# Spectral filter stage: every second group makes all eight filter steps in column tiles, between the sums

## The reference

```
def _stu_conv(phi, u, n):              # phi: (L, 16) filters, u: (b, sl, d)
    Vf = rfft(phi, n);  Uf_p = rfft(u, n);  Uf_m = rfft(u * sgn, n)
    U_plus  = irfft(Vf[None, :, :, None] * Uf_p[:, :, None, :], n)[:, :sl]
    U_minus = irfft(Vf[None, :, :, None] * Uf_m[:, :, None, :], n)[:, :sl] * sgn
def _compute_spectral(u, sigma, phi, Mpp, Mpm):
    s = sigma ** 0.25
    return einsum('btkd,k,kde->bte', U_plus, s, Mpp) + einsum('btkd,k,kde->bte', U_minus, s, Mpm)
def _stu(u, sigma, phi, Mu, Mpp, Mpm): return _compute_spectral(...) + _compute_ar_u(Mu, u)
t = t + _L1_ffn_ref(_ln_t(t), sigma, phi, M_u, M_phi_plus, M_phi_minus, log_weights, gumbel)
```

## Time and profile before

| | us |
|---|---|
| median of three runs | 1867.33 (1863.99 to 1873.28) |
| the profiled execution: its span, first to last instruction (the page gives no other time of it) | 1861.2 |
| median less span | 6.1 |
| TensorE matmuls busy | 1766.9, 95% of the span |
| VectorE busy / ScalarE busy | 1286.2 / 1178.1 |
| GpSimd busy | 623.4 |
| mean granted TensorE clock | 0.981 of full speed |

### The profile page before, as it was taken

How to read it: one execution, slowest core, us unless ns; L and a number is a source line. 1 busy time by engine, 2 the same in 40 slices (tenths; PEclk the granted TensorE clock), 3 DMA queues, 4 the chain that set the end, 5 groups by cost and what they waited for, 6 DMA issues and landing times.

```text
span 1861.2 us, 76300 instructions
## 1 busy us (share of the span) xinstructions
PE 1766.9 (95%) x32475; PEld 1389.6 (75%) x32475; DVE 1286.2 (69%) x3723; ACT 1178.1 (63%) x2555; POOL 623.4 (33%) x799
## 2 busy tenths in 40 slices
PE   5899999999999988989999999999999999999998
PEld 3567676666767656766788888888888888876665
DVE  2677778888877765373577777777777777647665
ACT  5788888888867654323677777777777777630000
POOL 6555555565545442030532213333312233100000
PEclk8999999999999989999999999999999999999999
DMA  4422333433232313598322122212221222277782
GB/s 118 114 79 74 103 85 92 111 90 100 71 105 77 96 52 115 140 224 197 119 60 62 38 67 68 67 47 68 57 58 43 68 67 64 79 184 205 208 207 70
DMA packets 266000, 183.74 MB, mean 99 GB/s; under 512 B 39888, under 2 KB 263022, under 8 KB 263868
## 3 DMA queue, kind: packets, MB, share of 16 engines
q1 hardware_dynamic: 262782, 177.29, 36.5%
q0 software_dynamic: 640, 1.16, 0.2%
q10 hardware_dynamic: 2240, 0.40, 0.1%
HBM read 108.26 MB, written 70.63 MB: 96 GB/s over the span
## 4 chain that ended last, share of the span: by engine, by line
PE 69%; DVE 10%; DMA 6%; issue 4%; POOL 4%; SPq 4%; ACT 3%; DVEq 0%; POOLq 0%; ACTq 0%
PE banks L1368 20%; PE banks L1346 10%; PE banks L1349 9%; PE banks L405 6%; DVE zone L606 3%; PE banks L1185 3%; PE banks L399 3%; SPq L1484 3%; PE banks L364 2%; PE banks L1180 2%; PE banks L354 2%; DMA zone<-Yd 2%; PE banks L412 2%; DMA YL<-Yd 2%; PE banks L1556 2%
## 5 line engine op out<-in xcount | busy, mean ns | idle before, releaser
L1401 DVE COPY Gm<-banks 128x448 f32<-128x448 f32 x896 | 552.8, 639 | 215.4 <-PE banks L1346 135.6
L1387 ACT ACTIVATE Gm<-banks 128x448 f32<-128x448 f32 x896 | 515.8, 629 | 189.9 <-PE banks L1346 144.3
L1368 PE MATMUL banks<-Gm,U 128*32 128x128 f32 x12544 | 515.0, 274 | 8.7 <-issue 7.9
L1368 PEld LDWEIGHTS banks<-Gm,U 128*32 128x32 f32 x12544 | 338.9, 110 | 51.6 <-issue 50.2
L1349 PE MATMUL banks<-V,zone 118*32 118x224 bf16 x7040 | 292.6, 259 | 0.2 <-issue 0.2
L1425 POOL COPY U<-UL 128x896 f32<-128x896 f32 (+2 forms) x28 | 50.1, 1788 | 545.9 <-PE banks L1368 441.0
L1346 PE MATMUL banks<-V,zone 118*128 118x224 bf16 x1824 | 215.0, 260 | 0.8 <-ACT qT L1196 0.6
L868 POOL TENSOR_TENSOR W<-W,mx 128x280 f32<-128x280 f32 x196 | 130.2, 664 | 226.2 <-DVE mx L655 224.9
L1349 PEld LDWEIGHTS banks<-V,zone 118*32 118x32 bf16 x7040 | 193.7, 96 | 0.8 <-issue 0.6
L1346 PEld LDWEIGHTS banks<-V,zone 118*128 118x128 bf16 x1824 | 157.0, 98 | 47.4 <-issue 39.3
L1556 PE MATMUL banks<-YC,zone 98*98 98x256 f32 x768 | 173.8, 387 | 3.8 <-DVE YC L1628 3.8
(11 more groups left out here) (164 smaller groups left out, 2545.6 us busy)
## 6 DMA issues: line engine op xcount, KB each, us to landing
Yd<-YS SPq DMA_DIRECT2D x112, 224.0 KB, 4.3
W<-Vd SPq DMA_DIRECT2D x392, 49.0 KB
zone<-Yd SPq DMA_DIRECT2D x32, 392.0 KB
YL<-Yd SPq DMA_DIRECT2D x32, 392.0 KB
UL<-Ud SPq DMA_DIRECT2D x27, 448.0 KB, 4.1
zone<-Mbf SPq DMA_DIRECT2D x28, 256.0 KB
Vd<-W SPq DMA_DIRECT2D x56, 112.0 KB
T<-XR SPq DMA_DIRECT2D x28, 224.0 KB, 2.6
```

Source lines behind the costliest of these rows:

```text
L1368: ins = e.matmul(p[32 * x:32 * x + 32, :], self.U7[(2 * P + ch) % 3][:, sl, 8 * (3 - q):8 * (3 - q) + 32], self.Gm[:, par, r:r + 2, :], st ...
L1387: e.activation(dst, src, ACT.Copy).then_inc(S["gm_act"], 1)
L1401: v.tensor_copy(dst, src).then_inc(S["gm_dve"], 1)
```

## The change

In groups 1 and 3 of each stage (`j % 2 == 1`) all eight steps are tiled, and they alternate with the parts of the sums: 0 1 p0 2 p1 3 p2 4 p3 5 p4 6 7 p5 p6. Groups 0 and 2 keep the run of four whole steps.

```diff
@@ Filters.order
-                out += step(0) + step(1) + step(2) + step(3) + part(0) + part(1) + step(4) + step(5) + part(2) + step(6)
-                out += part(3) + step(7) + part(4) + part(5) + part(6)
+                if j % 2 == 0:
+                    out += step(0) + step(1) + step(2) + step(3) + part(0) + part(1) + step(4) + step(5) + part(2) + step(6)
+                    out += part(3) + step(7) + part(4) + part(5) + part(6)
+                else:
+                    out += step(0) + step(1) + part(0) + step(2) + part(1) + step(3) + part(2) + step(4) + part(3) + step(5)
+                    out += part(4) + step(6) + step(7) + part(5) + part(6)
@@ Filters.tensor
-                whole = s == 0 or i % 8 < 4
+                whole = s == 0 or i % 16 < 4
```

## The result

The changed kernel takes 1896.62 us (median of four runs, 1889.06 to 1905.44) against 1866.03 for the kernel before on the same chip: a ratio of 1.0158, 95% interval 1.0136 to 1.018. It is slower, as forecast, by some 30 us where 20 were predicted, and inside the range. A second measurement (e11) gave a ratio of 1.0159 (1.0124 to 1.0194).

A forecast was written before the change was run, and what follows sets the result against it. TensorE's array was taken to bound the filter stages, and after the change its instruction supply: +17 us in place of -26 and +8, plus +3 for a long fetch, so 1867.3 + 20 = 1887 us, range 1847 to 1908.

The forecast's parts named there:

- The bound and its change-over: Filter stages: TensorE's array bounds them before the change, its instruction stream after it, at 13.73 us a stage.
- (1): Changed groups of the filter stages: whole steps become tiled, 0.24 us gained in each of 110 groups, -26 us.
- (2): Eviction slots: the third whole step after a changed group waits 0.07 us for its slot, +8 us (0 to +23).
- (3): TensorE's instruction supply in the filter stages: 3.39 packets a stage at 4.05 us each, +17 us, replacing array and slot terms.
- The long fetch near the end (+3 us): An instruction fetch such as that before 1614 us costs its whole excess, formerly partly covered by stored instructions; +3 us.
- The fetches are hidden: Rival: instruction fetches in the filter stages cost nothing from a 3.8 us spacing down; -18, 1849 us; chance 0.25.
- Supply at its lower end: Rival: instruction packets in the filter stages come every 4.2 us, +45, 1912 us; chance 0.07 beyond 1910.

The follow-up runs named there:

- e11: The changed kernel as it is, measured again on the same chip as the two runs with cut UL loads; ratio 1.0159 to the kernel before, 1898.45 us.
- e3: The changed kernel with each tiled filter matmul over 112 of its 224 columns, instructions and order the same; 1892.65 us.
- e4: The changed kernel with each whole filter matmul after stage 0 split into two of 112 columns; 1928.13 us.
- e1: The changed kernel with all four groups of a stage tiled and interleaved, no whole step after stage 0; 1946.72 us.
- e2: Groups 1 and 3 tiled as in the changed kernel, but steps and sums left in the old order; ratio 1.0112 to the kernel before.
- light loads: The changed kernel with UL loaded for one of four images from chunk 2 on, all instructions kept; 1884.27 us.
- e5: All steps after stage 0 in two column tiles of 64 instead of four of 32, in the changed groups' interleaved order; 2143.9 us.
- e7: The changed kernel with every store of YS made twice; ratio 1.0311 to the kernel before.
- e8: The kernel before with every store of YS made twice; ratio 1.0075 to the kernel before.
- e10: The kernel before with UL loaded for one of four images from chunk 2 on; ratio 0.9981 to the kernel before.

## Why the prediction was right

**The bound and its change-over.** That the stream of instructions takes over from the array held. e3 and e4 show it from both sides: less array work with equal instructions changes next to nothing, equal array work with more instructions costs what their packets cost. It held in the mean and not all the time, though: the prediction let the stream end last in every stage, but 36% of the pairs of groups ran at the pace of the array, and the late packets between them made the mean. That a fixed spacing times the packets still gave the stages to 1% is in part luck; for e1 the same product was 25 us too long (835 for 810.5).

**(1) and (2).** 2 x 3.32 + 2 x 3.08 + 2 x 0.07 = 12.93 us a stage was worked out; two undisturbed groups took 6.46, so 12.92. The slot wait, worked out with a delay from the first filter stage, was there at 0.05 to 0.07 us. The prediction let it vanish behind the stream; e2 leaves open whether it does (up to 9 us).

**(3), mis-sized by a few microseconds.** 868 instructions and 3.39 packets a stage: 187 packets in 55 stages, as counted. The spacing was put at 4.05 us; the profiled execution has 4.09, the repeat 4.11. 187 x 0.04 = 7 us, which is what is missing between 1881 and the span of 1887.8. The median of 1896.62 is 9.6 us above the forecast of 1887, 3 us more, because it stands 8.8 us above the profiled span where 6.1 were taken over from before. The spacing is no constant: 3.93 where array and slots want a packet every 3.28 us (e1), 4.04 with light loads, 4.27 with the doubled store. The mean over catching-up stretches of one execution was good to 1%, with luck: the scatter of those stretches was 3.65 to 4.27, and they had been picked by their late packets.

**The long fetch near the end (+3 us)** did not cost more where the prediction looked. Its stops of 1.99 and 1.35 us before came behind the two loads of the constants for the inverse transform (issued at 1606.7 and 1618.2 us); behind the same loads (1627.6 and 1637.8) the changed kernel has one stop of 1.99:

```profile
1645.52 0.35 PE L1353 MATMUL banks<-V,zone 118*32 118x224 bf16 x5 [1.99 <-issue]
```

The stop of 4.64 us is another one, behind the loads of `zone` from `Yd` at 1657 us, where the kernel before had none in its stages (its next, of 3.15 us, came in the last stage). The size of the term was right by chance.

**The rivals.** "The fetches are hidden" was wrong in its condition: half of the single spacings are near 3.8 us or below, but their mean over the stages never fell to it. "Supply at its lower end" (4.2 us) did not come either. The Trainium skill (page "Runtime: NRT & Kernel Launch", section "Instruction fetch mechanics") calls that cost mostly hidden; here 25 us of "issue" in 715 and e4's 28 us for 7 packets say that it is not, where array and slots want some 67 instructions per us. In the kernel before, at 58 per us, it nearly holds. The Trainium skill also says that a change of tiling mode drains TensorE (page "TensorEngine Tiling (Array Packing)", section "Key Properties"); e5's 0.13 us per change agrees.

**What stays open.** Why a packet takes some 3.8 us even with the data queues idle. In the stages of all traces no two packets begin less than 3.2 us apart, while one takes 1.1 us to carry, which fits one fetch at a time, each asked for when the last has landed. This was read off, not tested; no run changed the size of a fetch or the way in which fetches follow each other. Open too are the slots' share of the loss, at most some 9 us, and why e1 got its packets faster than e3 and e4.

## What to carry to other kernels

When TensorE runs many short matmuls, count its instructions beside its columns: divide the packets of its instruction queue into the time, and ask whether a change pushes that spacing to where late packets can no longer be made up for; in this kernel that was at some 4 us. A form that fills the array better but needs more instructions gains only until then, and the sign is idle time put down to "issue" in the middle of a row of equal matmuls. A few large matmuls that seem to waste a drain can be what lets the stream catch up (the excess of the spacing grows from 0.04 to 0.65 us as they go), and DMA traffic that no engine waits for can slow the supply.

## What was not expected of the hardware

- Matmuls in column tiles of 32 over 112 columns follow each other at 12.5 ns (e3). So the 25 ns from start to start that the Trainium skill gives as a floor (page "TensorE: Matmul & The Clock Gate", section "Wait — 56ns, not 53.3ns?") does not bound matmuls on different column tiles; this agrees with the 24 ns that the prediction took for 224 columns.
- Doubling the four stores of 224 KB per two stages, 25.7 MB in all, for which TensorE is not seen to wait, cost 29 us in one kernel and 14 us in the other (e7, e8).
- After the stop of 4.64 us the granted clock stood at half of full speed until 1672.5 us (the changed kernel), and in e10 too after stops of 2.86 and 2.52 us; after 3.15 us in the kernel before it did not. So a late packet can cost more than its stop.
- With late packets the runs of a kernel seem to scatter more: the standard deviation is 7.1 and 5.6 us for the changed kernel (four runs each time) and 2.9 to 4.2 for the kernel before (four sets of 4 to 16 runs).
